# Two graph layers over one dense adjacency: a first pass that sums x before projecting it, with three work buffers in place of two

## What is computed

```python
# adj: 4096 x 4096, x: 4096 x 256, f32 throughout
A = adj + eye(4096)
deg = sum(A, axis=1)
A_hat = A * rsqrt(deg)[:, None] * rsqrt(deg)[None, :]
x = layernorm(x + elu((A_hat @ x) @ w))            # layer 0
x = layernorm(x + relu((adj @ x) @ W.T + b))       # layer 1
```

## Time and profile before

| | |
|---|---|
| median of 3 runs (lowest, highest) | 886.92 us (886.02, 890.53) |
| the profiled execution, its own time | 887.87 us |
| its span, first to last instruction | 885.7 us |
| TensorE matmul busy | 793.4 us, 90% |
| VectorE busy | 740.4 us, 84% |
| ScalarE busy | 511.9 us, 58% |
| GpSimd busy | 189.3 us, 21% |
| read from HBM | 176.8 MB, 204 GB/s over the span |
| mean granted TensorE clock | 0.968 |

### The profile page before, as it was taken

How to read it: one execution, slowest core, us unless ns; L and a number is a source line. 1 busy time by engine, 2 the same in 40 slices (tenths; PEclk the granted TensorE clock), 3 DMA queues, 4 the chain that set the end, 5 groups by cost and what they waited for, 6 DMA issues and landing times.

```text
span 885.7 us, 10783 instructions
## 1 busy us (share of the span) xinstructions
PE 793.4 (90%) x3532; PEld 653.1 (74%) x3532; DVE 740.4 (84%) x611; ACT 511.9 (58%) x1132; POOL 189.3 (21%) x181
## 2 busy tenths in 40 slices
PE   0447959599999999899999999999999999999996
PEld 0335748477878888688888888888888888888884
DVE  2368878798989998698998999898989898888963
ACT  2254646465866564368876755756653765455351
POOL 0003341341344520012221101111210322022021
PEclk9967969899999999999999999999999999999998
DMA  9999987697799999879999977989896898997500
GB/s 273 306 307 292 215 156 174 163 248 186 168 268 283 186 225 215 189 185 213 225 211 210 243 207 197 193 218 194 205 245 197 182 249 183 220 219 178 130 24 25
DMA packets 183590, 181.71 MB, mean 205 GB/s; under 512 B 6768, under 2 KB 183536, under 8 KB 183536
## 3 DMA queue, kind: packets, MB, share of 16 engines
q1 hardware_dynamic: 94704, 93.21, 45.7%
q10 hardware_dynamic: 88832, 87.83, 42.6%
HBM read 176.82 MB, written 4.19 MB: 204 GB/s over the span
## 4 chain that ended last, share of the span: by engine, by line
PE 58%; DVE 1%; issue 0%; ACT 0%; POOLq 0%; POOL 0%; DVEq 0%; ACTq 0%
PE acc L972 18%; PE acc L974 18%; PE acc L973 18%; PE proj L931 3%; PE proj L929 1%; PE acc L952 0%; DVE v_lo L684 0%; DVE stats L837 0%; DVE raw L831 0%; PE acc L1004 0%; ACT v_hi L477 0%; ACT normed L610 0%; POOLq L173 0%; DVE mean_var L842 0%; POOL rstd L445 0%
## 5 line engine op out<-in xcount | busy, mean ns | idle before, releaser
L972 PE MATMUL acc<-a_hi,v_hi 128*128 128x512 f32 x1024 | 408.4, 399 | 43.2 <-DVE a_lo L643 27.6
L457 ACT ACTIVATE a_hi<-turned 128x1024 fp32r<-128x1024 f32 x256 | 264.5, 1058 | 277.6 <-PE acc L974 131.3
L973 PE MATMUL acc<-a_lo,v_hi 128*128 128x512 f32 x1024 | 403.4, 394 | 0.0
L974 PE MATMUL acc<-a_hi,v_lo 128*128 128x512 f32 x1024 | 403.1, 394 | 0.0
L643 DVE TENSOR_TENSOR a_lo<-turned,a_hi 128x1024 fp32r<-128x1024 f32 x256 | 313.1, 1258 | 42.8 <-ACT a_hi L457 32.4
L626 DVE STREAM_TRANSPOSE turned<-raw 128x2048 f32<-128x2048 f32 x122 | 280.0, 2302 | 8.5 <-DMA raw<-in_adj_dram 2.4
L972 PEld LDWEIGHTS acc<-a_hi,v_hi 128*128 128x128 f32 x1024 | 195.4, 191 | 87.3 <-issue 30.3
L974 PEld LDWEIGHTS acc<-a_hi,v_lo 128*128 128x128 f32 x1024 | 195.1, 191 | 41.4
L973 PEld LDWEIGHTS acc<-a_lo,v_hi 128*128 128x128 f32 x1024 | 195.3, 191 | 39.9
L467 ACT ACTIVATE acc<-raw 128x256 f32<-128x256 f32 x198 | 73.0, 368 | 23.0 <-DMA raw<-in_adj_dram 21.6
L418 POOL TENSOR_TENSOR raw<-raw,x_row 128x1024 f32<-128x1024 f32 x8 | 22.6, 2830 | 179.7 <-ACT raw L513 179.7
(11 more groups left out here) (69 smaller groups left out, 413.2 us busy)
## 6 DMA issues: line engine op xcount, KB each, us to landing
raw<-in_adj_dram SPq DMA_DIRECT2D x154, 512.0 KB, 9.5
raw<-in_adj_dram ACTq DMA_DIRECT2D x154, 512.0 KB, 10.0
x_row<-in_x_dram SPq DMA_DIRECT2D x64, 128.0 KB, 6.7
out_dram<-normed ACTq DMA_DIRECT2D x28, 128.0 KB, 3.2
held<-in_adj_dram ACTq DMA_DIRECT2D x4, 512.0 KB, 12.7
held<-in_adj_dram SPq DMA_DIRECT2D x4, 512.0 KB, 12.8
partial<-in_adj_dram ACTq DMA_DIRECT2D x2, 512.0 KB, 17.0
partial<-in_adj_dram SPq DMA_DIRECT2D x2, 512.0 KB, 18.5
```

Source lines behind the costliest of these rows:

```text
L457: nc.scalar.activation(a_hi[u % 2][:, part, :], turned[u % 2][:, part, :], ACT.Copy).then_inc(s_hi, 1)
L972: pe.matmul(dst, v_hi[:, k, ch], a_hi[u % 2][:, t, :], start=begin, stop=False)
L973: pe.matmul(dst, v_hi[:, k, ch], a_lo[u % 2][:, t, :], start=False, stop=False)
L974: ins = pe.matmul(dst, v_lo[:, k, ch], a_hi[u % 2][:, t, :], start=False, stop=end)
```

## The change

- **x summed first.** `turn_x`, `keep_xt` and `project_x` go. x is loaded into `x_in` (which lies where `v_lo` lies, 8 groups of it), y is x scaled by dinv, from SBUF. `project` of layer 0 now multiplies the sum by w, as layer 1 does by W. w, W and b are loaded at chunk 17 instead of chunk 1.
- **Loads first.** ScalarE issues its half of a chunk of pass A ahead of its units where the buffer is already free (`loads_first`).
- **Row sums.** Blocks of a chunk for VectorE, ScalarE, GpSimd: (8, 4, 4) in the first 8 chunks, (2, 6, 8) after, (5, 5, 6) in chunks 11 and 15. Before: (10, 6, 0) in the first 8, (6, 5, 5), then (3, 8, 5) and (4, 7, 5).
- **A unit turned inside each chain.** In chunks 3, 7, 11 and 15, which close a group row, one unit is turned between the row sums and `deg_sum`, and its low half is taken between `deg_row` and `y_low`.
- **Three buffers, low halves over turned units.** `turned` and `a_hi` have three buffers; `a_lo` is written over `turned`. So `turn(u)` waits until TensorE is done with unit u-3.
- The identity is added to a diagonal unit by one instruction instead of four. y is signalled tile by tile (`s_yhi`, `s_y`).

```diff
-    DVE_BLOCKS = [10, 10, 6, 3, 3, 4, 4, 4]
-    POOL_BLOCKS, POOL_FROM = 5, 2 * PANELS
+    EVEN, CLOSING, FIRST_ROWS = (2, 6, 8), (5, 5, 6), (8, 4, 4)
+    blocks_of = [FIRST_ROWS if n < 2 * PANELS else CLOSING if n < PANELS * FAST and n % PANELS == PANELS - 1 else EVEN
+                 for n in range(FIRST_B)]
+    ahead_of = {n: (visits[n] or visits[n + 1])[0] for n in range(PANELS - 1, PANELS * FAST, PANELS)}
...
+        freed = -1 if before[n] is None else done_at[before[n]]
+        if n < FIRST_B and freed < n - AHEAD:
+            loads_first[n - AHEAD].append(n)
+        else:
+            loads_at[max(n - AHEAD, freed)].append(n)
...
-        turned = [sb(f"turned{i}", [P, GT, GN]) for i in range(2)]
-        a_hi = [sb(f"a_hi{i}", [P, GT, GN], F32R) for i in range(2)]
-        a_lo = [sb(f"a_lo{i}", [P, GT, GN], F32R) for i in range(2)]
+        turned = [sb(f"turned{i}", [P, GT, GN]) for i in range(TURNS)]
+        a_hi = [sb(f"a_hi{i}", [P, GT, GN], F32R) for i in range(TURNS)]
+        a_lo = [nc.alloc_sbuf_tensor_at(f"a_lo{i}", [P, GT, GN], F32R, offset=turned_at + 4 * GT * GN * i) for i in range(TURNS)]
...
# SP, load_x
-                if m >= 1 and m <= GROUPS:
-                    sp.wait_ge(s_xw, m)
+                if FAST <= m < GROUPS:
+                    sp.wait_ge(s_turn, max(units_through[n] for n in HOMES))
+                elif m == GROUPS:
+                    sp.wait_ge(s_degp, FIRST_B)
...
# ScalarE, hi
-                    if u >= 2:
-                        act.wait_ge(s_used, halves_of(u - 2, half))
-                        act.wait_ge(s_lo, halves_of(u - 2, half))
+                    if u >= TURNS:
+                        act.wait_ge(s_used, halves_of(u - TURNS, half))
...
# ScalarE, make_y
-                act.wait_ge(s_xw, row + 1)
+                act.wait_ge(s_x, 64 * (row + 1))
...
# VectorE, turn
-                if u >= 2:
-                    dve.wait_ge(s_hi, halves_of(u - 2, 1))
-                    dve.wait_ge(s_lo, halves_of(u - 2, 1))
+                if u >= TURNS:
+                    dve.wait_ge(s_used, halves_of(u - TURNS, 1))
...
# VectorE, pass A
+                closing = row < FAST and at == PANELS - 1
+                if at:
+                    deg_of_pool(n - 1)
+                if closing:
                     raw_loaded(dve, n)
                     deg_part(n)
+                    turn_and_low(ahead_of[n])
+                    turned_through[0] = ahead_of[n] + 1
+                    deg_of_pool(n)
                     deg_sum(row)
+                    deg_row(row)
+                    low_and_later(ahead_of[n])
+                    y_low(row)
...
# VectorE, y_low
-                dve.wait_ge(s_vhi, row + 1)
+                    dve.wait_ge(s_yhi, GT * row + t + 1)
+                    nc.vector.scalar_tensor_tensor(out=v_lo[:, k, :], in0=x_in[:, k, :],
...
# TensorE, project
+                weights = w_sb if layer == 0 else wt_sb
                 for t in range(GT):
                     for h in range(CH):
-                        if layer == 0:
-                            ins = pe.transpose(proj[:, t, P * h:P * (h + 1)], nodes, ident[:])
+                        ins = pe.matmul(proj[:, t, :], agg[:, h, P * t:P * (t + 1)], weights[:, h, :],
+                                        start=(h == 0), stop=(h == CH - 1))
```

More of the change, by code:

```diff
@@ L341, in _ @@
                 if m <= GROUPS:
-                    n = PANELS * m + (1 if m < FAST else 2)
+                    n = PANELS * m + 2
                 else:
@@ L579, in _ @@
                     make_y(row - 1)
-                if not summed_first:
+                if not closing:
                     raw_loaded(act, n)
                     deg_part(n)
-                load_others(n)
-                if summed_first and n > PANELS:
-                    make_y(row)
-                if at == (2 if row < FAST else 3):
-                    keep_xt(row)
+                load_others(loads_at[n])
             for n in range(FIRST_B, len(chunks)):
@@ L891, in fold_degrees @@
                 ins.then_inc(s_dmm, 1)
-            def turn_x(row):
-                pe.wait_ge(s_x, 64 * (row + 1))
-                if row:
-                    pe.wait_ge(s_v, row)
-                flat = proj[:].rearrange("p t n -> p (t n)")
-                for h in range(CH):
-                    for t in range(GT):
-                        ins = pe.transpose(flat[:, GN * h + P * t:GN * h + P * (t + 1)], x_row[:, t, P * h:P * (h + 1)], ident[:])
-                ins.then_inc(s_xt_mm, 1)
-            def project_x(row):
-                pe.wait_ge(s_xt, row + 1)
-                flat = x_row[:].rearrange("p t n -> p (t n)")
-                for t in range(GT):
-                    for h in range(CH):
-                        ins = pe.matmul(proj[:, t, :], flat[:, GN * h + P * t:GN * h + P * (t + 1)], w_sb[:, h, :],
-                                        start=(h == 0), stop=(h == CH - 1))
-                ins.then_inc(s_xw, 1)
             def project(a):
@@ L979, in _ @@
                 row, at = divmod(n, PANELS)
-                if row < FAST and at == 2:
-                    turn_x(row)
                 if row < FAST and at == 3:
-                    project_x(row)
                     fold_degrees(row)
+                if n == WT_AT:
+                    turn_w()
                 for u in visits[n]:
@@ L988, in _ @@
                     product(u)
-                if row >= FAST and at == 2:
-                    turn_x(row)
-                if row >= FAST and at == 3:
-                    project_x(row)
             for u in range(visits[FIRST_B][0], U):
```

227 lines of the change are left out of this document (114 added, 113 removed).

## The result

The change makes the kernel slower: 916.29 us median (913.12 to 921.13, 4 runs) against 886.83 for the kernel before; the ratio is 1.033, 95% interval 1.027 to 1.039. The prediction said 868, with a range of 852 to 886. Its sign was wrong.

What follows compares the result with a forecast made beforehand. VectorE's list was to bound pass A, with u41 at 320.5 us, and TensorE the rest: 320.5 + 521.2 + 19.8 (w product) + 5 (buffers) = 866.5 span, giving 868 us against 886.9; range 852 to 886.

Steps and rivals of the forecast that it cites:

- y about 1.65: Price on VectorE's list up to u41: the four y_low instructions closing a group row take about 1.65 us together.
- No row of the trace before shows it, and my sum is made without it: GpSimd contention with y_low, now reading x from SBUF: 3 to 26 us by the skill's rule, left out of the sum.
- I take 0.74 a chunk: Low halves up to u41: VectorE loses 0.74 us per folded chunk to GpSimd's additions, against 0.33 before.
- the square: Scaling of the low halves' loss: chance to meet and time left both grow with GpSimd's additions, (4.4/2.95) squared.
- VectorE's list as the bound from u6 to u41: VectorE's work, with GpSimd meetings, sets u6 to u20 at 90 us and u20 to u41 at 128 us.
- the rival that starts from TensorE's pace: TensorE bounds pass A: u6 to u41 about 209 us instead of 218, second half loses nothing, 854 us; chance 17%.
- Chunk 7 lands about 58: Start of pass A: chunk 7's load lands at about 58 us, from 32 + 4 x 6.1 + 1.5.
- the product: From u41 on, layer 0's project multiplies by w instead of eight transposes, adding 19.8 us on TensorE.
- the buffers: From u41 on, three-buffer order delays VectorE by 0.6 us for each of layer 0's 8 rows: 5 us.
- The second rival: Behind u41, v_low and the layer-1 residual exceed VectorE's slack and TensorE stops: 33 us instead of 5, 896 us; chance 10%.
- VectorE and GpSimd collide more: Pass A: half the units caught, 30 us instead of 17; u41 at 335 to 340, 882 to 887 us; chance 11%.
- It doesn't do what it says: GpSimd's late additions hold buffers; u0 to u20 keeps 10 to 15 us of wait, 880 us; chance counted with first rival.

## Why the prediction was wrong

**What failed most: "y about 1.65", and "No row of the trace before shows it, and my sum is made without it".** The prediction named the mechanism and set it at nothing. `y_low` took 39.6 us for its 32 instructions instead of 15.2, so 24.4 us were missing, and taking them away alone gives 21 us at u41 and 15 us in all. The rule of the Trainium skill (GPSIMD Engine Reference, Key points), that GpSimd contends with VectorE instructions that read both operands from SBUF, is borne out: 1290 ns from SBUF, 474 from PSUM with the same GpSimd beside it. By the rule the sum was 3 to 26 us longer, and the measured 24.4 lies near the upper end. Two pieces of evidence were at hand and not used. The earlier trace rows show that a meeting costs the time of GpSimd's instruction, not a share of VectorE's: L384 ends at 187.22 and L387 at 189.05, and the two low halves end 1.08 us after them, at 188.30 and 190.13. For a 0.47 us instruction next to a 2.4 us addition that is a factor of five. And GpSimd's queue holds `make_dinv`, then the folds, in just the order that puts them beside `y_low` in the closings of group rows 0 to 3. All four were met, which is 17.8 of the 24.4 us; rows 4 and 5 make the other 6.6, and rows 6 and 7 lose nothing.

**Low halves: "I take 0.74 a chunk", 17 us.** Measured 26.1 us ((1514 - 1210) x 86), which over the 32 chunks that GpSimd now adds in is 0.82 each. The price was nearly right; the 17 us cover some 22 chunks only. Both factors behind the square did grow: 23 of the 86 low halves start during an addition, 17 in the kernel before, and lose some 1.1 us each where it was some 0.5. The row for the check, "low halves above 1.35 us mean", was met. Some 9 us.

**Folds that come late: not in the sum.** VectorE's finishing sums wait 9.0 us for GpSimd (7.5 in the rows above and 1.5 at the smaller form). They stood at 6.0 in the earlier trace rows, and the prediction dropped them with the rest of the waits. GpSimd's additions are themselves stretched by the meetings (L403 takes 3.28 us above against 2.40 alone), and its queue stands at `make_dinv`. Another 9 us.

**VectorE's list as the bound from u6 to u41: the list was right, the bound too low.** Without GpSimd's sums the list can be tested by itself. By the prediction's prices, with 1.07 us more for each chunk's row sums and 0.4 less for finishing, VectorE had 90 and 128 us to do between u6, u20 and u41; it was busy 88.4 and 125.9. But those stages took 91.7 and 139.5. In the last one VectorE is idle for 13.6 us: 5.4 for ScalarE's high halves, 3.8 for TensorE ahead of a turn, 4.4 ahead of the degree sums. And TensorE's list was itself too short in the prediction: u20 to u40 are 21 units, not 20, 114 us at 5.44 and not 109 (the rival that starts from TensorE's pace has the same slip), and TensorE was busy 122.3 us there at a granted clock of 0.95. Two engines nearly even at 126 and 122 of 139.5 us wait for each other in turn; the prediction set the longer list as the time. That the waits come from the lists being even is an argument from these numbers; no run tests it alone. Its own check, "VectorE over 95% busy u6 to u41", holds for the first of the two stages of the changed kernel (104.4 of 108.7) and fails for the second (133.5 of 149.6).

These four, 24 + 9 + 9 + 14, come to 56 us against the 54 that were missing. So close a match is partly luck: the last term (1.7 and 11.5 us over the two stages) is read from another version than the first three, and the terms overlap. What stands by measurement is that GpSimd's sums make 36.5 us at u41, net of the row sums that VectorE then does itself, and that moving `y_low`'s one operand to PSUM makes 21 us there.

**The start.** "Chunk 7 lands about 58": it landed at 62.5. Chunk 6 is in use from 51.74 after a wait for its DMA, so chunk 7 comes 10.8 us behind it, with x of group row 1 between, for which the prediction had 6.1 + 1.5; what the other 3 us are was not tested. VectorE's timeline, against the earlier trace rows:

```profile
33.65 2.29 DVE L661 TENSOR_REDUCE deg_parts<-partial 128x8 f32<-128x2048 f32 x1 [7.15 <-DMA partial<-in_adj_dram]
...
62.57 2.29 DVE L661 TENSOR_REDUCE deg_parts<-raw 128x8 f32<-128x2048 f32 x1 [7.86 <-DMA raw<-in_adj_dram]
```

Chunk 3 came at 33.6 for 32 predicted. From chunk 7's landing to u6 the version without GpSimd's sums takes 44.2 us, the changed kernel 53.8; 44.5 was predicted. The brake on SP went: its queue issues chunks 5 and 6 and then x of group row 1 from 25.9 to 44.1 without a gap, where it stood still from 36.5 to 42.3.

**What was right.** The whole stage from u41 on: 546.0 predicted, 544.6 measured, with the product (19.8; 16.6 to 21.1 by the runs) and the buffers (5; 2.7 and 5.8, though in other places). The turn in the chain. Loads first at nothing. The second rival, the loss behind u41 of 33 us, did not come.

**The rivals.** The first one, "VectorE and GpSimd collide more", was the cause, and even so its 882 to 887 us were 30 us short: it counted half the units caught and no `y_low`. Its check, "Wrong: u41 after 340", marks the outcome. The rival "It doesn't do what it says", with buffers held by late additions, did not come: no load is waited for behind chunk 7. The slower side was given 9%, all of it to another mechanism. A rival that takes the contention at its upper end in low halves and `y_low` together was never written down; with +44 and +26 both in the prediction's own text it would have stood at about 938 (868 + 44 + 26), and the measured 916 lies between.

**What stays open.** Why the high halves come later in VectorE's view without GpSimd's sums (6.8 us for 2.4) was not tried; ScalarE has ten blocks in place of six there, which would explain it, but no run separates it. How the loss grows between five and eight blocks is known at these doses only. What makes chunk 7 come 3 us late is open as well.

## What to carry to other kernels

Before handing work to GpSimd, list which VectorE instructions read both operands from SBUF, and see what GpSimd's queue will be doing when each of them runs: a queue that is held by a wait lets its backlog go right when the waited-for chain continues. Here that made 18 of `y_low`'s 24 us. Price a meeting by GpSimd's instruction, not by VectorE's, so that the short instructions on the critical chain are the ones most at risk; one operand in PSUM takes the risk away. And where two engines have nearly equal lists, take neither list as the stage's time: here 126 and 122 us made 139.5.
